# A static zero tile in front of each region, and a last tile moved back, in a spiral-convolution and mixture-of-experts block on one core

## The reference, cut to what matters

```python
x = x + attn_block(_layernorm(x))            # spiral convolution + SiLU MLP
logits = einsum('th,eh->te', xn, router_w)   # xn = _layernorm(x), t = 8192 tokens
topk_logits, topk_idx = top_k(logits, 2)
probs = softmax(topk_logits)
hmid = gelu(einsum('th,efh->etf', xn, w1) + b1[:, None, :])
y = einsum('etf,ehf->eth', hmid, w2) + b2[:, None, :]
x = x + xn + sum over the two chosen experts of prob * y
```

## Time and profile before

| what | us |
|---|---|
| median of 3 runs | 515.98 |
| lowest and highest of them | 512.52, 519.33 |
| the profiled execution | 512.49 |
| its span, first to last instruction | 510.7 |
| PE busy in the span | 404.6 (79%) |
| DVE, ACT, POOL busy | 350.7, 320.9, 276.0 |

### The profile page before, as it was taken

One profiled execution on the slowest core, in us unless ns is written; L12 is line 12 of the kernel. 1 busy time (PEld: TensorE's weight loads), 2 busy tenths in 40 slices (PEclk: granted clock), 3 DMA queues, 4 the chain that ended last, 5 costly groups with the idle time before them and its releaser, 6 DMA issues.

```text
span 510.7 us, 11454 instructions
## 1 busy us (share of the span) xinstructions
PE 404.6 (79%) x2813; PEld 354.7 (69%) x2813; DVE 350.7 (69%) x1318; ACT 320.9 (63%) x773; POOL 276.0 (54%) x341
## 2 busy tenths in 40 slices
PE   1362379898888989888976777859998998999990
PEld 1231259686858686757765766759998998999980
DVE  7999969969987989672625555526665766676761
ACT  5690567988867797746446423436776676777750
POOL 6607662647888886855252165444544444454442
PEclk9996579999998999889979785979999999999996
DMA  8540000000111111112023125653332332333200
GB/s 264 154 120 11 0 1 1 1 1 2 45 44 35 55 34 56 49 40 77 13 87 99 33 94 185 220 175 94 99 92 82 97 97 89 95 105 101 77 6 0
DMA packets 33284, 37.43 MB, mean 73 GB/s; under 512 B 5254, under 2 KB 29331, under 8 KB 33092
## 3 DMA queue, kind: packets, MB, share of 16 engines
q1 hardware_dynamic: 27236, 23.56, 15.7%
q0 software_dynamic: 5984, 13.13, 7.5%
HBM read 19.52 MB, written 18.92 MB: 75 GB/s over the span
## 4 chain that ended last, share of the span: by engine, by line
PE 46%; issue 13%; DVE 12%; POOL 8%; ACT 7%; SPq 4%; another core or an unknown queue 1%; DMA 0%; DVEq 0%; POOLq 0%; ACTq 0%
PE up_p L1020 13%; PE up_p L1037 7%; PE down_p L1037 6%; PE down_p L862 6%; POOL sorted_rows L587 4%; PE turn_p L834 4%; ACT rows L691 2%; SPq L426 2%; DVE stats L1123 2%; PE down_p L1029 2%; ACT work L664 2%; PE up_p L848 2%; PE route_p L900 2%; PE up_p L846 2%; PE up_p L847 1%
## 5 line engine op out<-in xcount | busy, mean ns | idle before, releaser
L621 POOL DMA_INDIRECT out<-result,out_id x91 | 89.5, 984 | 108.7 <-DVE result L1498 71.0
L793 ACT ACTIVATE hid_t<-up_p 128x512 f32<-128x512 f32 x91 | 54.3, 597 | 81.4 <-PE up_p L1020 64.8
L1020 PE MATMUL up_p<-xt,work 128*128 128x128 f32 x728 | 103.1, 287 | 2.1 <-issue 1.0
L587 POOL DMA_INDIRECT sorted_rows<-rows,pos x64 | 76.8, 1199 | 39.2 <-DVE pos L1240 22.4
L1020 PEld LDWEIGHTS up_p<-xt,work 128*128 128x128 f32 x728 | 93.5, 201 | 5.2 <-issue 3.5
L808 ACT ACTIVATE work<-mw_c 128x256 f32 x182 | 65.6, 416 | 1.1 <-issue 1.1
L862 PEld LDWEIGHTS down_p<-w_sb,work 128*128 128x128 f32 x512 | 61.5, 194 | 6.4 <-issue 5.7
L862 PE MATMUL down_p<-w_sb,work 128*128 128x128 f32 x512 | 64.4, 279 | 0.5 <-issue 0.5
L651 ACT ACTIVATE work<-up_p,b_all 128x512 f32<-128x512 f32 x64 | 41.5, 682 | 22.5 <-PE up_p L848 22.5
L834 PE MATMUL turn_p<-ident,work 128*128 128x128 f32 x192 | 29.9, 307 | 29.1 <-ACT work L677 11.7
L1037 PE MATMUL down_p<-mw_sb,hid_t 128*128 x368 | 51.8, 286 | 1.0 <-issue 0.5
(11 more groups left out here) (240 smaller groups left out, 804.4 us busy)
## 6 DMA issues: line engine op xcount, KB each, us to landing
tin<-sorted_rows SPq DMA_DIRECT2D x91, 136.0 KB
resid<-in_x SPq DMA_DIRECT2D x8, 512.0 KB, 3.7
sorted_rows<-zeros SPq DMA_DIRECT2D x29, 136.0 KB, 1.8
out<-result,out_id POOLq DMA_INDIRECT x91
work<-in_mw SPq DMA_DIRECT2D x1, 1024.0 KB, 6.1
sorted_rows<-rows,pos POOLq DMA_INDIRECT x64
work<-in_w SPq DMA_DIRECT2D x1, 256.0 KB
w_sb<-in_w SPq DMA_DIRECT2D x1, 256.0 KB
```

What stands on the lines that cost most here:

```text
L587: g.indirect_dma_start(sorted_dram, bass.IndirectOffsetOnAxis(pos[b % 2][:, j:j + 1], 0), rows[b % ROWBUFS][:, j, :], None).then_inc(s_sor ...
L621: g.indirect_dma_start(out_rows, bass.IndirectOffsetOnAxis(out_id[k][:, :], 0), result[k][:, :], None, bounds_check=TOKENS - 1, oob_is_err ...
L793: s_.activation(hid_t[s % 2][:, :], mid_p[s % 2][:, :], ACT.Gelu).then_inc(s_gelu, 1)
L1020: last = t.matmul(mid_p[s % 2][:, c * TILE:(c + 1) * TILE], ring[s % RING][:, c * 128:(c + 1) * 128], xt[s % 2][:, :], start=True, stop=True)
```

## The change

The buffer keeps its size and its regions, but each region's rows now begin 128 rows later (`spill_i`, which enters the positions, has base 128), and the 128 rows in front of each region, with those behind the last one, are set to zero by 29 stores with fixed addresses. They stand on SP behind the loads of x, where the store of the one zero tile stood. The pads, with their rows, registers, product on PE and addition on DVE, are gone. The table holds a first row in place of a tile's number. A region's last tile, if it has v < 128 rows, is moved back by 128 - v rows so that it ends with the region's last row: its first rows are then rows of the tile before it (or zeros of the tile in front), and `beyond` marks these first rows. That takes two more operations in `tile_table`.

```diff
-ZERO_TILE = NP * REGION // TILE
+ZERO_ROW = NP * REGION
-NOWHERE = 2 * ZERO_TILE
+NOWHERE = 2 * ZERO_ROW
...
-            sp.dma_start(sorted_tiles[ZERO_TILE, :, :], zeros[:, :]).then_inc(s_zero, 16)
-
-            def pads(pairs):
-
-                sp.load(pad_sp[0:len(pairs)], pad_at[0:1, pairs[0]:pairs[-1] + 1])
-                for k in pairs:
-                    at = sp.snap(pad_sp[k - pairs[0]], min_val=0, max_val=NP * REGION - TILE)
-                    sp.dma_start(sorted_dram[bass.ds(at, TILE), :], zeros[:, :]).then_inc(s_pad, 16)
+            for k in range(NP + 1):
+                sp.dma_start(sorted_dram[k * REGION:k * REGION + TILE, :], zeros[:, :]).then_inc(s_zero, 16)
...
-                    sp.wait_ge(s_zero, 16)
-                    sp.wait_ge(s_pad, 16 * NP)
+                    sp.wait_ge(s_zero, 16 * (NP + 1))
...
-                sp.dma_start(tin[s % INS][:, :], sorted_tiles[bass.ds(at, 1), :, :].rearrange("a p r -> (a p) r"))\
+                sp.dma_start(tin[s % INS][:, :], sorted_dram[bass.ds(at, TILE), :])\
...
-                if Tail.pads <= s < Tail.pads + NP // GROUP:
-                    if s == Tail.pads:
-                        sp.wait_ge(s_pad_at, 1)
-                    k = (s - Tail.pads) * GROUP
-                    pads(range(k, k + GROUP))
                 tile(s)
...
-                g.iota(spill_i[:, :], [[TILE, NP]], base=0, channel_multiplier=0)
+                g.iota(spill_i[:, :], [[TILE, NP]], base=TILE, channel_multiplier=0)
-                g.iota(region_i[:, :], [[REGION, NP]], base=0, channel_multiplier=0)
...
-                g.iota(row_i[:, :], [[TILE, TILES]], base=0, channel_multiplier=1)
-                g.iota(base_i[:, :], [[0, 1]], base=0, channel_multiplier=REGION // TILE)
+                g.iota(row_i[:, :], [[TILE, TILES]], base=TILE, channel_multiplier=-1)
+                g.iota(base_i[:, :], [[0, 1]], base=TILE - NOWHERE, channel_multiplier=REGION)
...
-                g.tensor_scalar(first_n[0:1, :], slot_i[0:1, :], 1.0, float(NOWHERE), ALU.mult, ALU.add)
-                g.tensor_copy(region_f[:, :], region_i[:, :])
+                g.tensor_scalar(first_n[0:1, :], slot_i[0:1, :], float(TILE), float(NOWHERE), ALU.mult, ALU.add)
...
-                if stage == 1:
-                    t.matmul(pad_p, ones_b[:, 0:1], before[b % 2][:, :], start=True, stop=True)
...
-                if stage == 1:
-                    d.tensor_tensor(pad_at[:, :], pad_p, region_f[:, :], ALU.add).then_inc(s_pad_at, 1)
...
-                d.tensor_scalar(facts[:, 0:1], shift_n[:, :], base_t[:, :], -float(NOWHERE), ALU.add, ALU.add)
+                d.tensor_scalar(facts[:, 0:1], shift_n[:, :], float(TILE), base_t[:, :], ALU.mult, ALU.add)
...
-                chain_t(d.tensor_tensor(beyond[:, 0:n], valid_p[:, 0:n], row_n[:, 0:n], ALU.is_le))
-                d.tensor_scalar(table[0:1, low_s:high_s], fact_n[0:1, 0:n], float(ZERO_TILE), None, ALU.min)
+                d.tensor_tensor(back_n[:, 0:n], valid_p[0:1, 0:n], row_n[0:1, 0:n], ALU.subtract)
+                chain_t(d.tensor_tensor(beyond[:, 0:n], valid_p[:, 0:n], row_n[:, 0:n], ALU.is_lt))
+                chain_t(d.scalar_tensor_tensor(out=fact_n[0:1, 0:n], in0=back_n[:, 0:n], scalar=0.0, in1=fact_n[0:1, 0:n],
+                                               op0=ALU.min, op1=ALU.add))
+                d.tensor_scalar(table[0:1, low_s:high_s], fact_n[0:1, 0:n], float(ZERO_ROW), None, ALU.min)
```

More of the change, by code:

```diff
@@ L178, in block_moe_kernel @@
         ones_b = sb("ones_b", [128, 128], bf16)
-        region_i = sb("region_i", [1, NP], i32)
         all_i = sb("all_i", [1, NP], i32)
@@ L195, in block_moe_kernel @@
         row_n = sb("row_n", [128, TILES])
-        region_f = sb("region_f", [1, NP])
-        pad_at = sb("pad_at", [1, NP], i32)
+        back_n = sb("back_n", [1, TILES])
         zeros = sb("zeros", [128, ROW])
@@ L231, in block_moe_kernel @@
         sorted_dram = nc.dram_tensor("sorted_rows", (NP * REGION + TILE, ROW), f32, kind="Internal").ap()
-        sorted_tiles = sorted_dram.rearrange("(n p) r -> n p r", p=TILE)
         def bank(name, k=1):
@@ L245, in block_moe_kernel @@
         count_p, sum_p = turn_p[0:NP, HALF:HALF + 1], turn_p[0:NP, HALF + 1:HALF + 2]
-        pad_p = turn_p[0:1, HALF + 64:HALF + 64 + NP]
         fact_p = turn_p[:, HALF + 128:HALF + 128 + TILES]
@@ L318, in block_moe_kernel @@
         s_zeros = sem("zeros_ready")
-        s_zero = sem("zero_tile_stored")
-        s_pad_at = sem("pad_rows_ready")
-        s_pad = sem("pads_stored")
+        s_zero = sem("zero_rows_stored")
         s_tc = sem("tile_counts_done")
@@ L392, in block_moe_kernel @@
             facts = 7
-            pads = 12
         def both_experts(packed):
@@ L438, in tile @@
                     sp.load(tile_sp[s // GROUP % 2][0:n], table[0:1, s:s + n])
-                at = sp.snap(tile_sp[s // GROUP % 2][s % GROUP], min_val=0, max_val=ZERO_TILE)
+                at = sp.snap(tile_sp[s // GROUP % 2][s % GROUP], min_val=0, max_val=ZERO_ROW)
                 after(sp, s_o, s - INS + 1)
-                sp.dma_start(tin[s % INS][:, :], sorted_tiles[bass.ds(at, 1), :, :].rearrange("a p r -> (a p) r"))\
+                sp.dma_start(tin[s % INS][:, :], sorted_dram[bass.ds(at, TILE), :])\
                     .then_inc(s_in[s % INS], 16)
             tile_sp = [[sp.alloc_register(f"tile_sp{q}{k}") for k in range(GROUP)] for q in range(2)]
-            pad_sp = [sp.alloc_register(f"pad_sp{k}") for k in range(GROUP)]
             sp.wait_ge(s_table, 1)
```

## The result

The changed kernel took 511.28 us (median of 4 runs, 507.72 to 513.55), the kernel before, run beside it, 517.62 us (512.52 to 519.33): ratio 0.9878, 95% interval 0.9828 to 0.9927. The mean of the four is 0.984, some 8 us. The ratios leave disturbed runs out and the medians don't, so the two need not agree to the last digit.

A forecast was written before the change was run, and what follows sets the result against it. PE bounds the steady tiles, but SP's queue of pad stores holds 308 to 340 us. The sum 10.1 - 2.3 - 0.3 = 7.5 us gave 505.0 against the profiled 512.49, so 508.5 against the 515.98 median; range 502 to 515.

The forecast's parts named there:

- The pads leave SP's queue: Behind tile 11, SP's pad stores no longer delay tile loads: 10.1 us gained up to tile 20, at most 13.1.
- Without that wait the last scatter would start at 333.1: POOL, batch 7: without its 2.92 us wait for tile 10's result, the last scatter starts at 333.1, not 335.75.
- rival B: Scatters, not pads, hold the stretch before tile 20; tile 20 at 341.2, gain 4.8 us, total 511.2; chance 0.28.
- row at 302 us: A 3.74 us "remote" wait up to 302.21, ahead of the first pad; the prediction's evidence that scatters hold the stretch.
- Tile 20's transpose comes at 338.5: On PE: last scatter, landing, SP's issue and load put tile 20 at 338.5, not 348.59: 10.1 us gained.
- The gap before tile 20 and its clock: PE waits 2.9 us before tile 20, and the lower clock behind it costs 2.3 us.
- C: Rival: pads hold all of the stretch, tiles run through without gap or lower clock; 12.8 us gained, 503.2; chance 0.21.
- Two operations more in each table: In tile_table on DVE: 0.3 us slower in the first table, bounds 0.2 and 0.5; nothing in the second.
- The zeros at 43 us cost nothing: 28 more SP stores from 43.33 us, 0.75 us each, issued by 64 us while SP is idle: no direct cost.
- D: Rival: the burst of zeros at 43 us delays engine handoffs, making the kernel slower, up to 530.7 us; chance 0.05.

The follow-up runs named there:

- e1: The changed kernel again, unedited, on another chip: 508.42 us, ratio 0.9778 to the kernel before.
- e8: The changed kernel again, unedited, on another chip: 512.36 us, ratio 0.9887 to the kernel before.
- e12: The changed kernel once more, unedited: 513.80 us, ratio 0.9825 to the kernel before.
- e4: The kernel before with 28 more stores of 136 KB at 43 us, to rows nobody reads: 519.29 us, ratio 1.0014.
- e9: The changed kernel with a 128x16 memset on POOL behind each indirect transfer up to tile 13: 503.04 us, ratio 0.9833 to the kernel before.
- e2: The changed kernel with the 29 zero stores in five groups behind the scatters of batches 0 to 4: 510.38 us, ratio 0.984 to the kernel before.
- e3: The changed kernel with 28 stores of 136 KB to scratch, four ahead of each load of tiles 12 to 18: 516.70 us, ratio 0.9987 to before.
- e6: The changed kernel with 28 scratch stores ahead of the loads of tiles 12 to 18, each 17 KB: 513.67 us, ratio 0.9861 to before.
- e11: The changed kernel with 128x16 POOL fillers up to tile 13 and batch 7's scatters two per tile: 507.25 us, ratio 0.9807 to before.
- e7: The changed kernel with batch 7's scatters issued two per tile (tiles 6 to 9), not one: 514.67 us, ratio 1.0021 to the kernel before.

## Why the prediction was right in its size and wrong in its reason

The forecast was 508.5 us, 7.5 below the 515.98 it started from. Measured were 6.3 us less on the first pair of kernels and some 8 over four pairs. The changed kernel's 511.28 lies inside the range, and in three of four measurements the gain was within 2%. The steps, one by one:

- **The pads leave SP's queue:** right. No store between 300 and 340 us, DMA at 89 GB/s, no tile that waits for a load.
- **"Without that wait the last scatter would start at 333.1":** the step that failed. The last scatter did not move: 63.9 us behind tile 0 in before, 64.2 in after, 62.9 in e1, 63.7 in e8, where the forecast put it 61.2 behind. It assumed that POOL's wait for the result of tile 10 (2.92 us) was the pads' doing. After the change POOL's timeline has 3.47, 3.68 and 3.21 us of such waits. They come of ACT's and DVE's late releases, which stayed, as rival B had it with its row at 302 us.
- **"Tile 20's transpose comes at 338.5":** 66.6 us behind tile 0 was forecast, 69.3 by B; measured 73.7, 71.1, 71.0 and 71.4 (e12), from 76.7 and 80.1 with the pads. The 10.1 us were 3.0 on the profiled pair, 5.3 to 5.7 against the other traces of after, and up to 9.1 if e4's trace stands for the pads. The path was another too: forecast and B both have tile 20 follow the last scatter by 5.4 us, and it came 6.4 to 9.5 us behind it, since the tiles ahead of it were late.
- **The gap before tile 20 and its clock:** absent in after, since the tiles ahead were late themselves. There the sign of C came true, but not C: PE was stalled by late releases and did not run through. In e9, where these are gone, the scatter (334.1), the tile (339.4) and the clock's loss are nearly what was forecast, though the gap is 7.52 us where 2.9 was: 343.26 - 339.40 = 3.86 us for tile 20 at a granted clock of 0.50, 2.0 over the steady 1.89, against the 2.3 charged. The working fits a kernel without late releases; after was not that kernel.
- **Two operations more in each table:** right. In DVE's timeline of after, table 1, the second costs one link, 264.87 to 265.07:

```profile
264.60 0.16 DVE L1274 TENSOR_TENSOR back_n<-turn_p,row_n 1x20 f32<-1x20 f32 x1
264.68 0.16 DVE L1275 TENSOR_TENSOR beyond<-turn_p,row_n 128x20 f32<-128x20 f32 x1
264.87 0.17 DVE L1276 SCALAR_TENSOR_TENSOR fact_n<-back_n,fact_n 1x20 f32<-1x20 f32 x1
265.07 0.16 DVE L1278 TENSOR_SCALAR table<-fact_n 1x20 int32<-1x20 f32 x1
```

- **The zeros at 43 us cost nothing:** right, and D is refuted by e4 (1.0014) and e2. Their size was off: 14.19 us for 29 stores, 0.49 each, where 0.75 was taken from stores with computed addresses. The landing hardly rose in the burst, from 1.8 us for the one store of before whose landing its trace has, the lone one at 43.33, to a median of 1.9 us with DMA at 237 GB/s from 50 to 60 us. The Trainium skill (DMA: Bandwidth & Descriptors, "Latency and other measured facts") gives a memory latency of 0.2 us on average and 2 us at high load; of such a rise this burst shows nothing.
- **Where the gain comes from, then:** e3 shows that it hangs on the stores between the tiles, and its trace shows no late load. That SP's queue was the whole of it, as forecast, doesn't hold; e6 leans to their traffic. On the trace of before the loads were late, so both may have had a part. How the traffic acts once no load is late stays open.

That the sum came out near the measured gain is in part luck. It counted 10.1 us up to tile 20, where the traces have 3.0 to 9.1, and it charged 2.3 for a gap that didn't come; the two errors lie against each other. It also placed all of the gain ahead of tile 20, while e3's loss, in its one trace, lies behind it.

The Trainium skill (SBUF — State Buffer, section "SBUF: two separate sides") says that a DMA cannot slow a compute operation, and that only DVE and GpSimd share a port, which ACT never waits for. The first part agrees with the late releases outliving the pads. By that rule the shared port can't be their cause, for ACT is released 5.42 us late beside DVE's 4.54; no run here tests the port itself.

## What to carry to other kernels

When a transfer is blamed for a stretch in which engines wait, look for the same kind of wait ahead of its first instance: the row at 302 us was the cheapest sign here, and it was right. Where POOL issues indirect transfers without a break for ten microseconds beside a chain of handoffs from PE to ACT and DVE, a tiny ordered instruction of its own between them is worth a try and a measurement (it cleared the late releases in three kernels and not in a fourth, and none of them was shown to be faster than the changed kernel), and putting more transfers in a row to "get them out early" may bring nothing. Count such waits from the end of the product that is waited for, and not from the profile's mark: by the mark e11 has two late ones, by the products seven. A forecast that hits its number is no proof of its working: check the intermediate times, here the last scatter.

## What the runs showed of the hardware that was not expected

- **Late releases stand beside rows of indirect transfers on POOL.** Products of PE ready at 315.10 and 316.11 were taken at 320.52 and 320.65, some 1.5 us behind the end of a row of seven; beside a row of nine (e7) the two came 7.07 and 7.17 us late; with a filler of 0.13 us between the transfers (e9) neither engine stood idle for over 2 us on a finished product, and tile 12 came 41.3 us behind tile 0, where it was 48.4. With the same filler e11 still had seven. By what path POOL's transfers reach a release from PE to ACT or DVE was not found.
- **What a store costs SP to issue varies with its surroundings:** 0.49 us each in the burst at fixed addresses; between the tiles 0.47 to 0.71 at fixed addresses (e3) and 0.53 to 0.87 at computed ones (before), so a fixed address is at best part of the difference.
- **The clock has its own alternatives:** the same code from 74 to 80 us ran at 1.00 in three of the executions profiled and at 0.51 to 0.67 in the others, and tile 0 came at 271.5 to 272.0 us with the one and at 273.8 to 277.6 with the other, in kernels with the change and without.
